# A graph network in 14 stages: the last groups' turns, copies and posts put at other places, 41 tiles cut as three and two, scatters divided anew

## What is computed

```python
h = relu(sage(x, W1l, b1l, W1r)); x = layernorm(x + sage(h, W2l, b2l, W2r))          # stages 0, 1
h = relu(gcn(x, W_conv, b_conv)); x = layernorm(x + h @ W_lin + b_lin)               # stage 2
h = relu(gcn(x, W1, b1));         x = layernorm(x + gcn(h, W2, b2))                  # stages 3, 4
w = dinv[src] * edge_attr * dinv[dst]
h = x
for l in range(3):                                                                   # stages 5 to 13
    out, x_ = h @ W[l, 0], h
    for k in range(1, 4):
        x_ = segment_sum(w[:, None] * x_[src], dst, N)
        out = out + x_ @ W[l, k]
    h = relu(layernorm(h + out + bias[l]) * gamma[l] + beta[l])
x = layernorm(x + h)
```

## Time and profile before

| | us |
|---|---|
| median of 3 runs | 8722.26 |
| lowest and highest | 8720.23, 8753.76 |
| profiled execution, its own time | 8723.8 |
| its span | 8721.9 |
| TensorE busy | 6499.0 (75%) |
| GpSimd busy | 4717.8 (54%) |
| VectorE busy | 2176.5 (25%) |
| ScalarE busy | 317.1 (4%) |

### The profile page before, as it was taken

How to read it: one execution, slowest core, us unless ns; L and a number is a source line. 1 busy time by engine, 2 the same in 40 slices (tenths; PEclk the granted TensorE clock), 3 DMA queues, 4 the chain that set the end, 5 groups by cost and what they waited for, 6 DMA issues and landing times.

```text
span 8721.9 us, 78855 instructions
## 1 busy us (share of the span) xinstructions
PE 6499.0 (75%) x26962; PEld 3819.1 (44%) x27153; DVE 2176.5 (25%) x8462; ACT 317.1 (4%) x856; POOL 4717.8 (54%) x4964
## 2 busy tenths in 40 slices
PE   0000069698867788887898888899888888888888
PEld 0000069345444444443554444455444444544444
DVE  8220034612212211111221113222121221212233
ACT  0000000000000000000000000000000000000000
POOL 3766710124554566564656656566565656656565
PEclk9999999899988898898998999899999999999998
DMA  9047000365546555554676666667666766666765
GB/s 361 5 182 294 0 0 0 92 193 161 155 117 206 170 182 156 158 180 163 241 252 234 242 232 248 230 241 244 244 245 239 253 235 231 242 234 243 247 249 208
DMA packets 582922, 1703.65 MB, mean 195 GB/s; under 512 B 163978, under 2 KB 326211, under 8 KB 480136
## 3 DMA queue, kind: packets, MB, share of 16 engines
q1 hardware_dynamic: 317434, 1337.93, 43.4%
q0 software_dynamic: 157744, 240.14, 9.4%
q10 hardware_dynamic: 107388, 120.98, 3.9%
HBM read 1476.48 MB, written 223.40 MB: 195 GB/s over the span
## 4 chain that ended last, share of the span: by engine, by line
PE 61%; another core or an unknown queue 17%; issue 15%; DVE 3%; DMA 3%; POOL 1%; DVEq 1%; ACT 1%; ACTq 0%; SPq 0%; POOLq 0%
PE pwide L1111 31%; PE pwide L1107 14%; PE pstep L1141 8%; PE pstep L961 5%; DMA counts<-lane_val,lane_idx 1%; PE pwide L1199 1%; DMA counts<-zz 1%; PE pwide L1157 0%; PE pwide L1198 0%; POOL weights L640 0%; DVEq L1502 0%; POOL ring_f L684 0%; DVE hot L1502 0%; POOL counts L640 0%
## 5 line engine op out<-in xcount | busy, mean ns | idle before, releaser
L684 POOL DMA_INDIRECT ring_f<-table,f_src x3492 | 3325.9, 952 | 2630.5 <-issue 944.3
L1111 PE MATMUL pwide<-room,acc 128*128 128x512 f32 (+1 forms) x3920 | 1871.0, 613 | 135.1 <-issue 128.7
L1111 PE MATMUL pwide<-room,hcur 128*128 128x512 f32 (+1 forms) x3136 | 1499.9, 615 | 110.5 <-issue 109.0
L1141 PEld LDWEIGHTS pstep<-hot,ring_f 128*128 128x128 f32 x7272 | 1049.8, 200 | 714.0 <-issue 640.4
L1141 PE MATMUL pstep<-hot,ring_f 128*128 128x64 f32 x7272 | 1016.7, 273 | 287.6 <-issue 264.0
L1681 DVE TENSOR_SCALAR hot<-iota,f_win,f_wgt 128x64 f32<-128x64 f32 x2916 | 718.9, 330 | 1944.4 <-remote 936.1
L1111 PEld LDWEIGHTS pwide<-room,acc 128*128 128x128 f32 x3920 | 735.8, 199 | 848.3 <-issue 802.0
L961 PE MATMUL pstep<-acc,hot 128*128 x2058 | 445.4, 349 | 833.0 <-issue 528.9
L1107 PE MATMUL pwide<-room 128*128 128x512 bf16 (+1 forms) x2652 | 989.1, 378 | 69.8 <-issue 65.5
L640 POOL DMA_INDIRECT counts<-lane_val,lane_idx x725 | 702.3, 969 | 401.2 <-issue 253.4
L1111 PEld LDWEIGHTS pwide<-room,hcur 128*128 128x128 f32 x3136 | 588.2, 199 | 681.7 <-issue 644.0
(11 more groups left out here) (316 smaller groups left out, 2482.4 us busy)
## 6 DMA issues: line engine op xcount, KB each, us to landing
room<-weights SPq DMA_DIRECT2D x700, 1024.0 KB
room<-counts SPq DMA_DIRECT2D x600, 512.0 KB
room<-weights SPq DMA_DIRECT2D x156, 768.0 KB
weights<-zz SPq DMA_DIRECT2D x56, 1792.0 KB
counts<-zz ACTq DMA_DIRECT2D x44, 1568.0 KB
ring_f<-table,f_src POOLq DMA_INDIRECT x3492
room<-weights SPq DMA_DIRECT2D x56, 512.0 KB
table<-acc ACTq DMA_DIRECT2D x56, 256.0 KB
```

The costliest lines, as they stand in the source:

```text
L684: pool.indirect_dma_start(out=ring_f[:, slot, :], out_offset=None, in_=rows_from[:, :], in_offset=bass.IndirectOffsetOnAxis(ap=f_src[:, c: ...
L1111: ins = pe.matmul(bank[:, 0:w * P], x_of(a)[:, first + o, :], room[:, n % SLOTS, o * w * P:(o + 1) * w * P], start=begins, stop=ends)
L1141: ins = pe.matmul(bank[:, low:low + WIN], row, one, start=begins, stop=ends and not own, skip_group_check=True)
```

## The change

- `Split` takes the distance of the last turn as a number of its own: `last=2` in `LATE`, so that group 12 turns at beat 140 and no longer at 142. In stages 1 to 4 it stays 4 or 8.
- The 41 dense tiles of stages 0 to 4 end with groups of three and two and no longer four and one. `starts` and `place_of` find a group's place where groups have any width, and two instructions in the prologue mend the addresses of the counts' scatters.
- On ScalarE `sums_out`, the copy of a group's sums, is cut out of `post`; where `soon` holds, the copy of the next group is made ahead of the Sqrt of this one. By the table this is group 5 in stage 4 and groups 2, 10 and 12 in `hop3` stages.
- On TensorE the posts of beats 0 and 1 of stage 5 (the last group of stage 4) stand ahead of its first dense row.
- The list of edges scattered into `weights` starts at chunk 300 and not 296, with 532 scatters in seven laps of 76 and not 536 in eight of 67; `QUOTA` is 161, 80, 150 and 141 and no longer 152, 80, 152 and 152.

```diff
-QUOTA = [0, 152, 80, 152, 152]
+QUOTA = [0, 161, 80, 150, 141]
...
-        order = [(-(-sum(dense[:k + 1]) * TILES * self.beats // self.mm) - 1, 0, self.ns + 4 * k, w, k)
+        order = [(-(-sum(dense[:k + 1]) * TILES * self.beats // self.mm) - 1, 0, self.ns + self.starts[k], w, k)
...
-        for o in self.order[1:]:
+        for o in self.order[1:-1]:
             self.turns.append(max(o[0] + 1, self.turns[-1] + gap))
+        self.turns.append(max(self.order[-1][0] + 1, self.turns[-1] + last))
...
+    def place_of(self, m):
+        k = sum(self.starts[i] * TILES <= m for i in range(1, len(self.dense)))
+        return k, m - self.starts[k] * TILES
...
-EARLY = Split([4, 4], [4] * 10 + [1], 12, 8)
-LATE = Split([4, 4, 4, 4, 2], [4] * 7 + [3], 9, -2)
+EARLY = Split([4, 4], [4] * 9 + [3, 2], 12, 8)
+LATE = Split([4, 4, 4, 4, 2], [4] * 7 + [3], 9, -2, last=2)
...
-LISTS.append(Lanes(296, CHUNKS, QS, LATE.ns * P, N))
+LISTS.append(Lanes(300, CHUNKS, 7, LATE.ns * P, N))
...
+            def soon(a, r):
+
+                p = SPLITS[a]
+                return KINDS[a] in (4, "hop3") and 0 < r < p.ng and p.order[r][0] <= p.turns[r - 1] + 1
...
+                if not soon(a, r):
+                    sums_out(a, r)
...
+                if soon(a, r + 1):
+                    sums_out(a, r + 1)
                 if kind in (1, 2, 4, "hop3"):
                     act.wait_ge(f_var, ln_turn(a, r) + 1)
                     act.activation(sd[:, 0:w], sd[:, 0:w], ACT.Sqrt).then_inc(f_sd, 1)
...
+                        if a == STAGES and b == 0:
+                            posts(BEAT0[a])
+                            posts(BEAT0[a] + 1)
                         for m in range(b * p.mm // p.beats, (b + 1) * p.mm // p.beats):
                             sweep(a, p, m)
-                        posts(BEAT0[a] + b)
+                        if a != STAGES or b > 1:
+                            posts(BEAT0[a] + b)
```

More of the change, by code:

```diff
@@ L67, with __init__ @@
 class Split:
-    def __init__(self, sparse, dense, lead=LEAD, trail=TRAIL, gap=GAP):
+    def __init__(self, sparse, dense, lead=LEAD, trail=TRAIL, gap=GAP, last=GAP):
         self.sparse, self.dense, self.lead, self.trail = sparse, dense, lead, trail
         self.ns = sum(sparse)
-        assert self.ns + sum(dense) == TILES and not any(w % 2 for w in sparse) and set(dense[:-1]) == {4}
+        assert self.ns + sum(dense) == TILES and not any(w % 2 for w in sparse)
+        self.starts = [sum(dense[:k]) for k in range(len(dense) + 1)]
         self.pairs = self.ns // 2
@@ L163, in pace @@
     m = p.beat_of(c // HB) * p.mm // p.beats
-    k, m = divmod(min(m, p.mm - 1), 4 * TILES)
+    k, m = p.place_of(min(m, p.mm - 1))
     ends = itertools.accumulate(o[3] * p.dense[k] for o in FROM[a].order)
@@ L780, in post @@
                 act.activation(zT, bank[:, 0:w * P], ACT.Copy).then_inc(z_done, 1)
+            def soon(a, r):
+                p = SPLITS[a]
+                return KINDS[a] in (4, "hop3") and 0 < r < p.ng and p.order[r][0] <= p.turns[r - 1] + 1
+            def post(a, r):
+                kind, G, p = KINDS[a], GROUP0[a] + r, SPLITS[a]
+                _, sparse_, first, w, k = p.order[r]
+                cols = slice(first, first + w)
+                x_to = x_of(a + 1)
+                zT = zT4[G % 2][:, 0:w, :].rearrange("p t d -> p (t d)")
+                hT = hT4[G % 2][:, 0:w, :].rearrange("p t d -> p (t d)")
+                if not soon(a, r):
+                    sums_out(a, r)
                 if turns_back(kind):
@@ L1082, in sweep @@
             def sweep(a, p, m):
-                k = min(m // (4 * TILES), len(p.dense) - 1)
+                k, done = p.place_of(m)
                 w, at = p.dense[k], DENSE_AT[a, k]
-                o, j = divmod(m - 4 * TILES * k, w)
+                o, j = divmod(done, w)
                 u = 0
@@ L1091, in sweep @@
                 bank = dense_bank[at % 2]
-                begins, ends = m == 4 * TILES * k, m == 4 * TILES * k + w * TILES - 1
+                begins, ends = done == 0, done == w * (TILES - 1)
                 if begins and at >= 2:
@@ L1102, in sweep @@
                     return
-                ends = m == 4 * TILES * k + w * (TILES - 1)
                 if a < STAGES:
@@ L1113, in sweep @@
                 if ends and own:
-                    ins = selves(a, bank, p.ns + 4 * k, w)
+                    ins = selves(a, bank, p.ns + p.starts[k], w)
                 if o == nb - 1:
@@ L1328, in place @@
                 link(V.tensor_scalar(l_dst, l_dst, float(-(LATE if which == NC else EARLY).ns * P), None, ALU.add))
+                if which == NC - 1:
+                    link(V.tensor_scalar(l_dst2, l_dst, float(EARLY.starts[-2] * P), float(P), ALU.is_ge, ALU.mult))
+                    link(V.tensor_tensor(l_dst, l_dst, l_dst2, ALU.add))
                 link(V.tensor_tensor(l_dst, l_dst, l_f1, ALU.subtract))
```

11 lines of the change are left out of this document (4 added, 7 removed).

## The result

The changed kernel takes 8643.7 us (median of four runs, 8639.1 to 8661.12); the kernel before took 8733.96 with the runs made beside it (four, 8720.23 to 8753.76). The ratio is 0.9905, with a 95% interval of 0.988 to 0.993: 83 us faster, between 61 and 105. The forecast was 8673 in a range of 8620 to 8716. The sign and the range held, but the gain is larger than the 50 us of the sum, and about half of it comes from stages to which the sum gave 4.

The account below looks back on a forecast made before the run. TensorE's multiplies were taken as the path, its idle and half-clock time as what could be won. Terms -13 -12 -3.4 -5 -10 -3 -4 +1 -1 gave -50 us from the median of 8722.26: 8673, range 8620 to 8716.

Parts of the forecast that it names:

- Copies and the end: ScalarE's copies ahead of the Sqrt: -3 us in stage 7, -7 in stage 13; VectorE's idle at the end: -3.
- Turns: Last group two beats sooner: stage 8 -13 us, stage 11 -12, stage 13 -3.4, from waits, half clock and earlier pauses.
- the gathers begin 5 us sooner: At weighted stage boundaries: the last group's `mixed` runs six dense rows (5.2 us) sooner, so GpSimd's gathers start 5 us sooner.
- the pause comes at gather 30: Stages 8 and 11: GpSimd first pauses after 30 gathers, not 36, cutting 7.5 us of slow TensorE; 5 us won each.
- Stage 4 to 5: Posts moved into TensorE's wait for the first weighted load; gathers start some 10 us sooner: -5 us, bounds -6 and +1.
- 41 tiles: Last dense groups of three and two: -4 us of waits for counts, +1 for one more tile to mix at stage 2.
- Scatters: Four fewer scatters, nine more in stage 1, eleven fewer in stage 4: -1 us, bounds -4 and +4.
- late signals: Signals that come late with GpSimd's scatters, taken as all that a scatter costs, since GpSimd is busy 307 of 522 us.
- Only the waits: Rival: pause stays at gather 36, no clock regained, copies no sooner; 20 us won, 8702; chance 0.22.
- too soon: Rival: sums not ready at the earlier beat, TensorE's dense work stands behind in nine weighted stages; +51 us, 8773; chance 0.07.
- The bad phase shrinks in all weighted stages: Rival: earlier gathers pause at gather 24, six fewer in the slow state in nine stages; -45 us more, 8628; chance 0.10.
- A floor for narrow matmuls: Rival: 128-column passes wait 0.10 us for weight loads, so wider tiles win 32 us more in five stages; 8641; chance 0.06.

Follow-up runs that it names:

- after: The changed kernel with the whole change in, against the kernel before: 8643.7 us, ratio 0.9905.
- the paced tail: Changed kernel, with the 40 scatters behind a stage's last gather also waiting for TensorE's use of loads, two per load: 8561.0 us, ratio 0.980 to the kernel before.
- the pause at the 13th gather: The paced tail, plus the 13th gather of each weighted stage waiting until TensorE has used eight loads: ratio 0.9795 to the kernel before.

## Why the prediction was right in sign and too small

- *Copies and the end* (-13 in the sum): right. The waits of the earlier trace rows are gone, and undoing brings the end's 2.88 us back. That the whole 13 were won is not shown: stage 13 is 7 to 15 us longer with the old copies in one kernel and not in another (507.4 us).
- *Turns* (-28 at stages 8, 11 and 13): the mechanism is right up to VectorE, and the size was off. The step that failed is "the gathers begin 5 us sooner": from the last send to the first gather of stage 8 are now 6.4 us, not 3.5, so 2 to 4 us are won at the boundaries; the closer sends may be the cause, which is not shown. 8.8 of 13.3 us of waits went. That the pause comes at gather 30 held in after but is no rule (seven times of twelve in the other kernels with new turns), and in after a second pause follows at 36. What the part is worth is open: 30 us by profiled executions, which differ by as much with the same weighted code, and nothing that the ratios can tell.
- *Stage 4 to 5* (-5): the first gathers came 8 us sooner, as forecast within 2, and no gain is seen by stage 6's first gather (539.2 and 539.7 us); executions differ too much there to confirm 5 us or to rule them out.
- *41 tiles* (-4 and +1): the waits for counts went as said, and the old cut brings 5.3 us of them back. Stage 4 is 18 us longer with it, 8 of them where it passes into stage 5, where a gain is not seen to last; the rest is not explained by a row.
- *Scatters* (-1, bounds -4 and +4): the step that failed most. It was priced at GpSimd's time, which the stage hides, and at "late signals" that I took to be spread evenly. Undoing costs 34 us up to the first float32 matmul (which the kernels with old turns, old copies and old posts, whose scatters are the new ones, reach at 4009 to 4026) and 33 by the ratios. What scatters cost is TensorE's own time, by its lower clock and, where they stand in an unbroken row, by instructions that are held: up to the first float32 matmul TensorE is at the lower clock for 588 us before, 534 after, 584 with the old scatters and 419 with the paced tail.
- *Rivals.* "Only the waits" (8702) and "too soon" (8773) are out by the time; the waits of group 12's posts on ScalarE never came, since its copy stands 7 us ahead. "The bad phase shrinks in all weighted stages" did not happen: its first pause is never sooner than gather 30. "A floor for narrow matmuls" (8641) is nearest to the measured 8643.7, and the rows rule it out: the time alone would have chosen a wrong cause.
- *Luck.* The sum of 50 came near because one term too large (the weighted part, 46 for 36) met one far too small (4 for 40). The range reached from 6 to 102 us below the 8722 of the kernel before and would have held without either error, so that it held proves little of the terms.

What stays open: why the state begins and why it holds other engines' instructions; why two scatters change the clock of stage 3; what the weighted part's 36 us are made of; and the 10 us of the cut within stage 4.

## What to carry to other kernels

Where the profile shows an engine issuing one instruction at a time with idle that nothing ends, look at what another engine was doing without a pause just then, and try to break that row with a wait that costs it nothing: three lines were worth as much here as a retimed schedule. Before calling an idle engine stopped, look what its next instruction waits for. Price work on an engine that is not the bound by the path's state beside it, not by the engine's own busy time. And when a send is moved ahead, measure up to the reader: of the 5.1 us that VectorE won at stage 8, 2.9 were lost between the send and the first gather.

## What the runs showed of the hardware

A row of GpSimd's indirect transfers at 1.25 to 1.27 us each, with nothing but 0.30 us between them, is followed after 12 to 21 us by a state in which other engines run ready instructions late: in stage 4 of after TensorE one matmul of 384 columns each 2.80 us and not each 0.16, and ScalarE a copy 42.6 us after its last signal; in stage 6 with the pause at the 13th gather ScalarE a copy 26 us late. It ends some 6 us behind the row. With pauses of 1.4 to 2.0 us every 4 to 18 us most of it is gone (TensorE's idle times behind the last gather 4 to 19 us a stage, 34 to 44 without). It isn't the scatter as such (the same 40, paced, leave TensorE busy for two thirds of the time), and it isn't the place in the program (one pause of 4.84 us moves it by a row of gathers). The lower clock goes with it: 0.52 and 0.65 in the stretches above. Why ready instructions are held no run here shows.
